# Turning the stacks of q and k by rounded-format matmuls instead of 32-bit transpositions

## The reference, cut to what matters

```
x = x + tanh(g_xattn[0]) * xattn(layernorm(x), ctx, ctx)      # 32 query heads, 8 key/value heads, D = 16
x = x + tanh(g_ffn[0])   * ffn(layernorm(x), ...)             # shared expert 1408 wide, 32 experts, top 4

xattn: qh = q.reshape(B, S, 8, 4, 16)      kh = k.reshape(B, S, 8, 16)      vh = v.reshape(B, S, 8, 16)
       weights = softmax(qh . kh / 4)      out = weights . vh
```

## Time and profile before

| | |
|---|---|
| median of the runs | 2277.96 us |
| the profiled execution, its own time | 2276.01 us |
| its span in the trace | 2274.2 us |
| attention phase at its steady pace | about 60 to 680 us |
| PE, DVE, ACT, POOL busy over the span | 96%, 68%, 52%, 29% |

### The profile page before, as it was taken

How to read it: one execution, slowest core, us unless ns; L and a number is a source line. 1 busy time by engine, 2 the same in 40 slices (tenths; PEclk the granted TensorE clock), 3 DMA queues, 4 the chain that set the end, 5 groups by cost and what they waited for, 6 DMA issues and landing times. The chain is left out here.

```text
span 2274.2 us, 53961 instructions
## 1 busy us (share of the span) xinstructions
PE 2192.4 (96%) x17121; PEld 1842.6 (81%) x17121; DVE 1539.9 (68%) x3135; ACT 1178.4 (52%) x2363; POOL 651.8 (29%) x1553
## 2 busy tenths in 40 slices
PE   6999999999997999999999999899999999999999
PEld 4777777777775888988889888798988989888888
DVE  6999999999996886556556556665555545455554
ACT  5888888888885433333333343433333333333332
POOL 5777777777773100000000003200000100001000
PEclk9999999999998999999999999999999999999999
DMA  3555555555554213443434435324243334344431
GB/s 82 144 141 139 147 142 134 147 143 136 143 151 125 68 65 129 147 147 110 143 120 138 141 116 174 130 96 137 84 138 92 115 101 137 98 153 157 155 104 65
DMA packets 318827, 286.25 MB, mean 126 GB/s; under 512 B 123265, under 2 KB 236929, under 8 KB 318722
## 3 DMA queue, kind: packets, MB, share of 16 engines
q1 hardware_dynamic: 314370, 272.23, 39.5%
q0 software_dynamic: 4352, 12.65, 2.1%
HBM read 195.43 MB, written 88.34 MB: 125 GB/s over the span
## 5 line engine op out<-in xcount | busy, mean ns | idle before, releaser
L1401 PE MATMUL p_a<-x_h,ws_h 128*128 128x256 f32 x1280 | 377.2, 295 | 17.3 <-ACT term L1137 10.1
L1402 PE MATMUL p_a<-x_l,ws_h 128*128 128x256 f32 x1280 | 363.0, 284 | 0.0
L1403 PE MATMUL p_a<-x_h,ws_l 128*128 128x256 f32 x1280 | 362.7, 283 | 0.0
L1115 ACT ACTIVATE chosen<-chosen 128x256 f32<-128x256 f32 x352 | 146.3, 417 | 394.2 <-DVE chosen L1319 213.0
L595 DVE TENSOR_REDUCE negmax<-p_max 128x8 f32<-128x1024 f32 x256 | 312.7, 1221 | 46.6 <-PE p_max L747 42.6
L1424 PE MATMUL acc<-wd_h,hh 128*128 128x512 f32 x704 | 277.0, 393 | 4.1 <-DVE rows L1339 3.3
L1401 PEld LDWEIGHTS p_a<-x_h,ws_h 128*128 128x128 f32 x1280 | 245.0, 191 | 38.5 <-ACT term L1137 14.2
L473 ACT ACTIVATE probs<-p_exp 128x1024 f32<-128x1024 f32 x256 | 261.3, 1021 | 27.2 <-PE p_exp L697 20.9
L1425 PE MATMUL acc<-wd_l,hh 128*128 128x512 f32 x704 | 274.9, 390 | 0.0
L1426 PE MATMUL acc<-wd_h,hl 128*128 128x512 f32 x704 | 274.5, 390 | 0.0
L1357 DVE TENSOR_TENSOR chosen<-p_b,term 128x256 f32<-128x256 f32 x176 | 74.7, 424 | 254.3 <-PE p_b L1403 153.1
(11 more groups left out here) (199 smaller groups left out, 5378.4 us busy)
## 6 DMA issues: line engine op xcount, KB each, us to landing
rows<-out_dram SPq DMA_DIRECT2D x32, 1024.0 KB, 6.4
x_raw<-xn_cols SPq DMA_DIRECT2D x124, 256.0 KB, 2.9
out_dram<-rows SPq DMA_DIRECT2D x31, 1024.0 KB, 4.3
ew<-in_L_ffn_Wg_dram SPq DMA_DIRECT2D x32, 704.0 KB, 6.2
ew<-in_L_ffn_Wu_dram SPq DMA_DIRECT2D x32, 704.0 KB, 7.5
xs<-in_x_dram SPq DMA_DIRECT2D x64, 256.0 KB, 2.7
xres<-in_x_dram SPq DMA_DIRECT2D x64, 256.0 KB, 2.9
out_dram<-x SPq DMA_DIRECT2D x64, 256.0 KB, 2.6
```

The costliest lines, as they stand in the source:

```text
L1115: nc.scalar.activation(act_g[:, cols], gate[:, cols], ACT.Silu).then_inc(silu2_done if half else silu1_done, 1)
L1401: mm(bank, w_h[:, a, k, :], x_h[:, b, k, :], start=start and k == 0, stop=False, skip_group_check=not start)
L1402: mm(bank, w_h[:, a, k, :], x_l[:, b, k, :], start=False, stop=False, skip_group_check=not start)
L1403: last = mm(bank, w_l[:, a, k, :], x_h[:, b, k, :], start=False, stop=(k == 1), skip_group_check=not start)
```

## The change

`ks` and `qs` are declared in the rounded format, so the casts of their high parts fall away and the rests are now rounded as POOL writes them (ACT rounded them later before). A second identity in the rounded format, `ident_r`, is made by ACT at the start. `k_cols` and `q_cols` call the ordinary matmul with the stack as weights and `ident_r` as the moving operand, in place of the transposition. Every other call of TensorE keeps its transposition or matmul, and no instruction changes its place.

```diff
-            ks = sb("ks", [128, NKV, 64])
+            ks = sb("ks", [128, NKV, 64], F32R)
-            qs = [sb(f"qs{i}", [128, NC, G, 2, 64]) for i in range(2)]
+            qs = [sb(f"qs{i}", [128, NC, G, 2, 64], F32R) for i in range(2)]
+            ident_r = sb("ident_r", [128, 128], F32R)
...
-                    nc.gpsimd.tensor_tensor(ks[:, :, 32:48], kin, ks[:, :, 16:32], ALU.subtract).then_inc(ks_done, 1)
+                    nc.gpsimd.tensor_tensor(ks[:, :, 32:48], kin, ks[:, :, 16:32].bitcast(F32), ALU.subtract).then_inc(ks_done, 1)
...
-                        last = nc.gpsimd.tensor_tensor(stack(3, g2), heads(g2), stack(1, g2), ALU.subtract)
+                        last = nc.gpsimd.tensor_tensor(stack(3, g2), heads(g2), stack(1, g2).bitcast(F32), ALU.subtract)
...
             @block.scalar
             def _(act):
+                act.wait_ge(consts, 1)
+                nc.scalar.activation(ident_r[:, :], ident[:, :], ACT.Copy).then_inc(ident_r_set, 1)
                 act.wait_ge(g_in, 32)
...
             @block.tensor
             def _(pe):
                 pe.wait_ge(consts, 1)
+                pe.wait_ge(ident_r_set, 1)
...
                     for c in range(NC):
-                        last = tr(p_pv[:, 128 * c:128 * c + 128], ks[:, 2 * c:2 * c + 2, :].rearrange("p g r -> p (g r)"), ident[:, :])
+                        last = mm(p_pv[:, 128 * c:128 * c + 128], ks[:, 2 * c:2 * c + 2, :].rearrange("p g r -> p (g r)"), ident_r[:, :],
+                                  start=True, stop=True)
...
                     for i in range(G):
-                        last = tr(p_tq[:, 128 * i:128 * i + 128], qs[b.par][:, c, i, :, :].rearrange("p g r -> p (g r)"), ident[:, :])
+                        last = mm(p_tq[:, 128 * i:128 * i + 128], qs[b.par][:, c, i, :, :].rearrange("p g r -> p (g r)"), ident_r[:, :],
+                                  start=True, stop=True)
```

More of the change, by code:

```diff
@@ L208, in build @@
             spare_d, spare_p, spare_s = sem("spare_d"), sem("spare_p"), sem("spare_s")
-            consts, tanh_done = sem("consts"), sem("tanh_done")
+            consts, tanh_done, ident_r_set = sem("consts"), sem("tanh_done"), sem("ident_r_set")
             pads, id0 = sem("pads"), sem("id0")
@@ L353, in k_stacks @@
                     kin = kv[b.par][:, :].rearrange("p (g d) -> p g d", d=D)
-                    nc.gpsimd.tensor_scalar(ks[:, :, 16:32].bitcast(F32R), kin, 1.0, 0.0, ALU.mult, ALU.add)
-                    chain.inc(nc.gpsimd.tensor_scalar(ks[:, :, 48:64].bitcast(F32R), kin, 1.0, 0.0, ALU.mult, ALU.add))
+                    nc.gpsimd.tensor_scalar(ks[:, :, 16:32], kin, 1.0, 0.0, ALU.mult, ALU.add)
+                    chain.inc(nc.gpsimd.tensor_scalar(ks[:, :, 48:64], kin, 1.0, 0.0, ALU.mult, ALU.add))
                     chain.wait(pool)
-                    nc.gpsimd.tensor_tensor(ks[:, :, 32:48], kin, ks[:, :, 16:32], ALU.subtract).then_inc(ks_done, 1)
+                    nc.gpsimd.tensor_tensor(ks[:, :, 32:48], kin, ks[:, :, 16:32].bitcast(F32), ALU.subtract).then_inc(ks_done, 1)
                 def q_stacks(b):
@@ L372, in q_stacks @@
                         for g2 in range(2):
-                            last = nc.gpsimd.tensor_scalar(stack(part, g2).bitcast(F32R), heads(g2), 1.0, 0.0, ALU.mult, ALU.add)
+                            last = nc.gpsimd.tensor_scalar(stack(part, g2), heads(g2), 1.0, 0.0, ALU.mult, ALU.add)
                     chain.inc(last)
@@ L509, in _ @@
                 for i in range(2):
-                    nc.vector.memset(qs[i][:, :, :, :, 0:16], 0.0).then_inc(pads, 1)
+                    nc.vector.memset(qs[i][:, :, :, :, 0:16].bitcast(F32), 0.0).then_inc(pads, 1)
                 nc.vector.memset(kt[0][:, :, :].bitcast(F32), 0.0)
                 nc.vector.memset(kt[1][:, :, :].bitcast(F32), 0.0).then_inc(pads, 1)
-                nc.vector.memset(ks[:, :, 0:16], 0.0).then_inc(dve_chain, 1)
+                nc.vector.memset(ks[:, :, 0:16].bitcast(F32), 0.0).then_inc(dve_chain, 1)
                 chain = Count(dve_chain)
@@ L516, in _ @@
                 chain.wait(dve)
-                nc.vector.memset(ks[:, :, 0:1], 1.0).then_inc(pads, 1)
+                nc.vector.memset(ks[:, :, 0:1].bitcast(F32), 1.0).then_inc(pads, 1)
                 dve.wait_ge(id0, 3)
```

## The result

The changed kernel takes 2281.41 us (18 runs, 2279.99 to 2282.95) against 2277.57 us for the kernel before (18 runs beside it). The ratio is 1.0016, with a 95% interval of 1.0009 to 1.0024: 3.8 us slower, real but under the 0.2% that was called telling. The prediction said 2278.5 us, between 2268 and 2291.

The account below looks back on a forecast made before the run. At the attention phase's steady pace no engine was free, PE and DVE waiting for each other. Terms of -2.6, +3.2 and -0.5 us gave about 0, so 2278 us, stated as 2278.5, range 2268 to 2291.

Parts of the forecast that it names:

- The tie of the steps: In q_cols and k_cols, a rounded matmul's step would equal a transposition's, 0.109 us; no step changing was given 0.57.
- the half microsecond on top: Added to the forecast of 2278 us because the upper bound of the step was held nearer than the lower.
- A step stays at 0.109: Term 1: the 20 q and k steps a batch keep 0.109 us, now set by the load; 0 us.
- The rival with the plain 32-bit rate: Narrow rounded q and k matmuls cost 0.22 us each, +115 to +141 us, 2393 to 2419 us; chance 0.16.
- the one with 0.12 a step: Rival: q and k loads put each step at 0.12 us, +9 us, 2287 us; chance 0.12.
- o_cols starts 0.04 us sooner behind k_cols, -2.6 us: Term 2: the last k matmul streams only 0.07 us, so o_cols starts sooner, on the path at c = 3.
- The longer first load behind the maxima, +3.2 us: Term 3: q_cols at c = 0 and 2 shows 0.05 us more load at one of the two places.
- Matmuls end 0.05 us sooner: Term 4: a group's last matmul lasts 0.22 to 0.23 us against 0.273, so ACT reads earlier; 0 to -1 us.
- The expected row of 0.55 us for four q matmuls: Sign in the profile after: four q matmuls in mid-stream take 0.55 us in place of 0.60.
- POOL's rounding is free: Term 5: POOL's rounded rests cost 0.01 to 0.03 us each, hidden by its 0.8 us wait a batch.
- The bound from below: If loads hide, steps fall to 0.07 us, saving 50 us on PE, of which at most 28 us show.
- the smaller of the faster cases: Only terms 2 and 4 tell, at c = 3 and q evacuations: -5 to -8 us, 2271; all faster cases 0.15.

Follow-up runs that it names:

- e5: Changed kernel with each rounded matmul of 128 columns split into two of 64, weights loaded for each; 2402.70 us (single run).
- e2: Changed kernel with only the k steps as rounded matmuls and q transposed again; 2275.49 us, 0.9998 of the kernel before.
- e7: Changed kernel with rounded ks, qs and the new identity kept, but all stacks turned by transpositions; 2276.26 us, 0.9998 of the kernel before.
- e1: Changed kernel with rounded matmuls and transpositions alternating within each group of four; 2275.40 us, 0.9995 of the kernel before.
- e6: Changed kernel with only the first of each group of four a rounded matmul, the others transpositions; 2276.01 us, 0.9996 of the kernel before.
- e10: Changed kernel with rounded matmuls for k and the q groups behind o_cols, q behind the maxima transposed; 2276.00 us, 1.0005 of the kernel before.
- e9: Changed kernel with rounded matmuls for k and the q groups behind the maxima, q behind o_cols transposed; 2278.37 us, 1.0012 of the kernel before.

## Why the prediction was right

The tie of the steps came out, and with it the time. That the time is a little longer was no result of the sum, which gave about 0; the half microsecond on top was a lean. One term was mis-sized, by 1.8 us, and one of some 2.2 us was missing; the range took them in.

1. *A step stays at 0.109.* Right, with 0.111 to 0.113 measured, and for the reason given: e5 doubled the loads and got 0.111 us for each. The growth of 0.002 was not in the term. The rival with the plain 32-bit rate is refuted by the first profile, the one with 0.12 a step as well. Both rules of the Trainium skill that were weighed ("TensorE: Matmul & The Clock Gate", sections Terms and "Weight-path perf modes") would have moved a step. The rounded format showed neither a cost four times as high nor a faster load.
2. *o_cols starts 0.04 us sooner behind k_cols, -2.6 us.* Mis-sized. From the load ahead of k_cols to the last load of o_cols the median went from 1.115 to 1.103 us, 0.012 us less, or 0.8 us over 64: the k steps themselves grew a little and the rest of the gain is smaller. In e2 none of it reached the pace.
3. *The longer first load behind the maxima, +3.2 us.* This is the term that carries the loss of pace. Right in kind and near in size. One of the two places shows it, as the term says: the stretch grew by 0.056 us at c = 2, where 0.05 was taken, and by 0.014 at c = 0. The pace shows 0.04 of it, 2.4 us.
4. *Matmuls end 0.05 us sooner.* Only where the load is hidden (221 ns). ACT still waits 0.5 us in 200. The expected row of 0.55 us for four q matmuls was wrong for this reason, it is 0.64; the expected loads, 190 ns each and 0.52 us for four, were right.
5. *POOL's rounding is free.* Right: 957 ns for 256 columns, against 956 in the same stretch before; e7. ACT's copy stood at 2.04 us and took 0.31 us.
6. *Missing: the start.* Some 2.2 us go with a clock that rises later. The prediction looked at the granted clock only at the steady pace. With the loss of pace over the other 55 batches, 2.1 us, that makes 4.3 us, where 3.8 were measured with an interval of some 2 to 5.5.

The bound from below is not borne out. It let a saving on PE show up to 28 us, what DVE waits for p1. e1 and e6 saved 0.08 and 0.04 us a batch on PE, 5 and 3 us over 64, and won nothing that shows. Larger savings were not tested. And the smaller of the faster cases, "-5 to -8 us" from terms 2 and 4, doesn't follow from them: they add up to -2.6 to -3.6 us.

## What to carry to other kernels

Work out load and streaming of a matmul apart, from a row after a wait and from two widths. Here a form that halved the streaming and doubled the load changed nothing in a stream, and cost its longer load where PE had just waited. Where another matmul's streaming covered the load it cost nothing (e10), behind a wait it did (e9). Before counting a wait as a gain to be had, check with a small cut whether the pace follows: here the waiting engine's own instructions grew by what it had waited less. And look at the first 30 us apart from the loop.

## What the hardware showed that was not expected

- At the level of 2.4 GHz a rounded load of 128x128 takes 0.111 us from its start to the next load (e5), and a transposition's 0.058 us after a wait; the streaming of 128 columns takes some 0.06 us (by the start of the second k matmul's record) and 0.109 us. Behind another rounded matmul, one that waits for its load reads 272 to 277 ns in place of 221.
- The rise of the clock at the start seems to vary with what PE runs: 19.2 to 26.5 us with transpositions, 32.1 to 32.4 with rounded matmuls, and 53.2 us with halves of 64 columns (e5). From the first kind to the second the ninth batch comes 2.2 us later. Ahead of each rise PE had run at the level of 1.2 GHz since its first matmul at 10.9 to 11.1 us. Why rounded matmuls delay it is open; no run here tells.
- Where rounded matmuls and transpositions alternate, a pair takes 0.20 us (e1), more than the 0.07 and 0.109 us of streaming that were expected to set it, and less than two steps of 0.11.
